# A gated cross-attention kernel on one core: the projections' matmuls spread over the whole attention

## What is computed

```python
# layer 0: cross-attention, 16 heads of 16, with pruned columns
q, k, v = ln(x) @ Wq.T + bq, ctx @ Wk.T + bk, ctx @ Wv.T + bv
s = softmax(q @ k.T / 4)                  # per head, 512 x 512
keep = top_k(s.sum(over queries), 460)    # 52 of 512 columns are dropped
x = x + tanh(g) * ((s * mask(keep)) @ v) @ Wo.T
x = x + tanh(g) * fp4_mlp(ln(x))          # 704 hidden, 16-element blocks
# layer 1: attention without softmax: q (k'v) needs only one 256 x 256 matrix
x = x + ...ln(x) @ (Wq1 @ blockdiag(k'v))...
x = x + tanh(g) * int8_linear(ln(x))
```

## Time and profile before

| | |
|---|---|
| median of 3 runs | 1215.02 us |
| times of the runs | 1215.01, 1215.02, 1220.33 us |
| span of the profiled execution | 1211.1 us |
| its busy time: TensorE, VectorE, ScalarE, GpSimd | 997.9, 1013.7, 935.9, 163.6 us |

### The profile page before, as it was taken

The page is one execution under the profiler, slowest core; times in us unless marked ns, Lnnn a source line. Parts: engine busy times, 40 slices in busy tenths (PEclk is TensorE's granted clock), DMA queues, the critical chain, the costliest instruction groups (busy, mean ns, idle before and its releaser), DMA issues.

```text
span 1211.1 us, 17973 instructions
## 1 busy us (share of the span) xinstructions
PE 997.9 (82%) x5672; PEld 476.7 (39%) x5672; DVE 1013.7 (84%) x2009; ACT 935.9 (77%) x2135; POOL 163.6 (14%) x183
## 2 busy tenths in 40 slices
PE   7888999967777677777777778998999999999974
PEld 5554556511111111111111111335677777767652
DVE  6887677788889888889888887567999999999965
ACT  5456565489999999999999998776567667766744
POOL 2221231020000000000000000101232222222212
PEclk9999999989999999999999999989999999999985
DMA  9730653042211222111223101101111211110001
GB/s 308 180 114 1 200 149 104 19 123 38 39 27 34 45 45 45 33 31 29 44 46 80 33 20 35 37 9 40 53 36 36 62 44 36 49 48 27 18 18 35
DMA packets 77906, 71.80 MB, mean 59 GB/s; under 512 B 13754, under 2 KB 71412, under 8 KB 77812
## 3 DMA queue, kind: packets, MB, share of 16 engines
q1 hardware_dynamic: 77812, 70.65, 22.2%
HBM read 42.83 MB, written 27.28 MB: 58 GB/s over the span
## 4 chain that ended last, share of the span: by engine, by line
PE 42%; ACT 39%; issue 9%; DVE 9%; DMA 0%; POOL 0%; ACTq 0%; DVEq 0%
ACT ea L1322 19%; ACT prob L1336 15%; PE ps_a L1598 13%; PE ps_b L1556 8%; PE ps_v L1556 3%; DVE nmax L1223 2%; PE ps_c L1571 2%; PE ps_a L1607 2%; PE ps_c L1632 1%; PE ps_v L1195 1%; PE ps_b L760 1%; PE ps_v L735 1%; PE ps_b L701 1%; PE ps_b L1146 1%; PE ps_c L1179 1%
## 5 line engine op out<-in xcount | busy, mean ns | idle before, releaser
L1322 ACT ACTIVATE ea<-ps_a,nmax 128x512 f32<-128x512 f32 x512 | 362.7, 748 | 72.2 <-DVE nmax L1223 72.2
L1223 DVE TENSOR_REDUCE nmax<-ps_a 128x2 f32<-128x1024 f32 x256 | 313.7, 1225 | 52.7 <-PE ps_a L1146 51.4
L1336 ACT ACTIVATE prob<-ps_b 128x1024 f32<-128x1024 f32 x214 | 236.1, 1103 | 0.0
L1146 PE MATMUL ps_b<-q_st,k_st 52*128 52x512 f16 x512 | 105.8, 391 | 137.7 <-ACT prob L1336 129.6
L1146 PEld LDWEIGHTS ps_b<-q_st,k_st 52*128 52x128 f16 x512 | 26.1, 93 | 364.2 <-ACT prob L1336 303.9
L1598 PE MATMUL ps_a<-wgu,xT 128*128 128x352 f32 x512 | 166.2, 465 | 3.4 <-ACT xT L1761 2.1
L1195 PE MATMUL ps_v<-prob,v_in 128*16 128x512 f32 x1024 | 135.5, 600 | 11.9 <-DVE att L1290 11.5
L1179 PE MATMUL ps_c<-ea,rz 128*32 128x512 f32 x1024 | 137.2, 608 | 0.0
L1322 ACT ACTIVATION_READ_ACCUMULATOR ea<-ps_a,nmax 128x1 f32 x512 | 135.8, 265 | 0.0
L1598 PEld LDWEIGHTS ps_a<-wgu,xT 128*128 128x128 f32 x512 | 92.9, 191 | 48.9 <-issue 7.0
L1773 ACT ACTIVATE ea<-ps_a 128x352 f32<-128x352 f32 x128 | 59.7, 467 | 59.1 <-PE ps_a L1598 58.7
(11 more groups left out here) (279 smaller groups left out, 1685.8 us busy)
## 6 DMA issues: line engine op xcount, KB each, us to landing
k_scr<-k_p SPq DMA_DIRECT2D x24, 256.0 KB, 2.9
q_scr<-q_p SPq DMA_DIRECT2D x24, 256.0 KB, 2.8
q_st<-q_scr SPq DMA_DIRECT2D x32, 192.0 KB, 4.8
k_st<-k_scr SPq DMA_DIRECT2D x32, 192.0 KB, 5.0
c_in<-in_ctx SPq DMA_DIRECT2D x8, 512.0 KB, 4.4
x_in<-in_x SPq DMA_DIRECT2D x8, 512.0 KB, 5.9
v_scr<-v_s SPq DMA_DIRECT2D x8, 512.0 KB, 3.1
v_in<-v_scr SPq DMA_DIRECT2D x16, 256.0 KB, 3.2
```

Source lines behind the costliest of these rows:

```text
L1146: return e.matmul(bank, left[b][o:o + rows, r, t * P:t * P + P], right[b][o:o + rows, r], start=True, stop=True)
L1223: e.tensor_reduce(nmax[u % 2][:, t].rearrange("p (h r) -> p r h", h=2)[:, r], ps_a[:, z % 2 * 2:z % 2 * 2 + 2], AX_X, ALU.max, negate=True ...
L1322: e.activation(ea[c % RING][:, g % 4], ps_a[:, g % 4], ACT.Exp, bias=nmax[u % 2][:, t, n:n + 1], accum_out=tot[u % 2][:, t, n:n + 1]).then ...
L1336: e.activation(dst, ps_b[:, :, :], ACT.Exp).then_inc(s_prob, 1)
```

## The change

Five things are changed together.

1. A fill is now done on TensorE in parts: X1, Q, K and V in two, GRAM in four, the others whole. Of the 187 parts that follow the first twenty fills, 67 are spread over half steps 0 to 40 (BEFORE, OPEN), and 120 over half steps 41 to 211, 0.7 per half step (RATE). Parts from z = 41 on use one bank of their own, `ps_f`. ScalarE empties a fill that ends at z at its step z - 1 (`leaving`), VectorE at step z (`ended`), GpSimd at z.
2. Column sums and values share one bank, `ps_s`: sums in partitions 0 to 63, values in 64 to 127. In every half step two matmuls of the sums and two of the values are issued, next to each other, where before four of the one or of the other were. The values' operand is 32 columns wide and half zeros (`v_pad`), written by GpSimd (`pad`).
3. ScalarE writes Q and K with their bias as float32 (`full`), and GpSimd splits them (`halves`: a copy and a subtraction, both 128x512). VectorE's `low_part` is gone.
4. `second` comes a half step later (z - 43), and ahead of the sums and values in TensorE's step. On VectorE the copy of the values moves to the head of a step, and the reciprocals go ahead of the ranking.
5. Buffers and DMA order: one `c_in` instead of two, one `q_p`, `k_p`, `v_s`, `m_s`; three `prob` instead of four; SP goes half step by half step, and loads a unit's heads 6 half steps ahead of their use. The dropped columns take 2 DMAs a unit instead of 4, the results 4 instead of 8. Fp4 work is dealt out over other fills of batches 1 to 3.

The core of the diff:

```diff
+    BEFORE, RATE = 67, 0.7
+    def bank_of(s):
+        return s % BANKS if s < alone else BANKS - 1
+    def parts(n):
+        if n >= 0 and n % FILLS in (X1, Q0, Q1, K0, K1, V0, V1):
+            return 2
+        return 4 if n >= 0 and n % FILLS == GRAM else 1
+    pieces = [(s, part) for s in range(AHEAD, len(SEQ)) if real(SEQ[s]) for part in range(parts(SEQ[s]))]
+    def turn_of(j):
+        if j < BEFORE:
+            return j * OPEN // BEFORE
+        return OPEN + int((j - BEFORE) / RATE)
...
+        def halves(dst, x, c, b, stored, done):
+            if b:
+                e.wait_ge(stored, OUT * b)
+            e.tensor_copy(dst[:, 0, c], x).then_inc(*po.up())
+            e.wait_ge(*po.now())
+            e.tensor_tensor(dst[:, 1, c], x, dst[:, 0, c], ALU.subtract).then_inc(done, 1)
...
-        def high_part(src, dst, bias, c):
-            return e.activation(dst[:, 0, c], src, ACT.Identity, bias=bias[:, c:c + 1])
+        def with_bias(src, n, bias, c):
+            j = QK.index(n)
+            for done, kinds in ((s_pool_q, (Q0, Q1)), (s_pool_k, (K0, K1))):
+                earlier = sum(x % FILLS in kinds for x in QK[:max(j - 1, 0)])
+                if earlier:
+                    e.wait_ge(done, earlier)
+            e.activation(full[j % 2][:, :], src, ACT.Identity, bias=bias[:, c:c + 1]).then_inc(s_act_full, 1)
...
+        def column_sums(g, k):
             u, n = g // GROUPS, g % GROUPS
+            t, r = n % TT, n // TT
             e.wait_ge(s_recip, g + 1)
+            if n == 0 and k == 0:
                 e.wait_ge(s_rank, u)
-            for j in range(4):
-                e.matmul(ps_c[32 * j:32 * j + 32, :], rz[:, n % TT, n // TT, j], ea[g % RING][:, j],
-                         start=(n == 0), stop=(n == GROUPS - 1)).then_inc(s_colsum, 1)
+            o = FIRST_ROW - 2 * r - k
+            for h in range(2):
+                e.matmul(ps_s[32 * h:32 * h + 32, :], rz[:, t, r, 2 * k + h, o:o + 32], ea[g % RING][:, 2 * k + h],
+                         start=(n == 0 and k == 0), stop=(n == GROUPS - 1 and k == 1)).then_inc(s_colsum, 1)
+        def values(g, k):
+            e.wait_ge(s_prob, 2 * g + k + 1)
+            if n == 0 and k == 0:
+                e.wait_ge(s_pad, u + 1)
+            if t == 0 and k == 0:
+                e.wait_ge(s_att, g // TT)
+            for h in range(2):
+                o = SUMS + 32 * h
+                e.matmul(ps_s[o:o + 32, :], v_pad[u % 2][:, t, 4 * r + 2 * k + h], at.prob[g % PROBS][:, 2 * k + h],
+                         start=(t == 0 and k == 0), stop=(t == TT - 1 and k == 1)).then_inc(s_value, 1)
         def step(z):
             if z < ALL_Z:
                 first(z)
-            if z % 2:
-                g = within((z - 5) // 2, ALL_G)
-                if g is not None:
-                    column_sums(g)
-            else:
-                g = within((z - LAG - 4) // 2, ALL_G)
-                if g is not None:
-                    values(g)
-            b = within(z - LAG, ALL_Z)
+            b = within(z - LAG - 1, ALL_Z)
             if b is not None:
                 second(b)
+            g = within((z - 4) // 2, ALL_G)
+            if g is not None:
+                column_sums(g, z % 2)
+            g = within((z - LAG - 4) // 2, ALL_G)
+            if g is not None:
+                values(g, z % 2)
...
+        def ended(z):
+            return pj.ends_at.get(z, ())
+        def leaving(z):
+            return [*(ended(z) if z <= pj.open else ()), *(ended(z + 1) if z >= pj.open else ())]
...
             for z in range(at.last):
                 step(z)
-                for n in fills(z):
-                    fill(n)
+                for s, part in pj.at_turn.get(z, ()):
+                    fill(s, part)
```

More of the change, by code:

```diff
@@ L177, in build @@
         fp4 = tiles.fp4
-        at = attend(m, w, scr, tiles)
+        at = attend(m, w, scr, tiles, fp4)
+        with ExitStack() as early:
+            fp4.wide_tiles(Mem(nc, early, ctx))
+        at.prob = [m.sb(f"prob{n}", [P, 4, T]) for n in range(at.probs)]
         with ExitStack() as early:
@@ L697, in transposes, with fill @@
             return ins
-        def into(dst, n, src, oc):
-            for ic in range(DC):
-                ins = e.matmul(dst, wt[:, n, ic, oc * P:oc * P + P], src[:, ic], start=(ic == 0), stop=(ic == DC - 1))
-            return ins
-        def fill(s):
-            n, dst = SEQ[s], bank[s % BANKS]
+        def fill(s, part):
+            n, dst = SEQ[s], bank[bank_of(s)]
             if not real(n):
                 return
-            g = s - BANKS
-            while g >= 0 and not real(SEQ[g]):
-                g -= BANKS
-            if g >= 0:
+            g = before(s)
+            if g >= 0 and part == 0:
                 e.wait_ge(*left(SEQ[g]))
@@ L717, in fill @@
             p = b % 2
+            last = part == parts(n) - 1
             if k in (CT0, CT1):
@@ L746, in fill @@
                 e.wait_ge(s_act_cT, 2 * b + 2)
-                into(dst, WK, cT, k - K0).then_inc(s_pe_k, 1)
+                oc = k - K0
+                ins = e.matmul(dst, wt[:, WK, part, oc * P:oc * P + P], cT[:, part], start=(part == 0), stop=last)
+                if last:
+                    ins.then_inc(s_pe_k, 1)
             elif k == KV:
@@ L787, in fill, with whole, stats, variances @@
                 e.wait_ge(s_act_xT, 2 * b + 2)
-                into(dst, WQ, xT, int(k == Q1)).then_inc(s_pe_q, 1)
-        return fill
+                oc = int(k == Q1)
+                ins = e.matmul(dst, wt[:, WQ, part, oc * P:oc * P + P], xT[:, part], start=(part == 0), stop=last)
+                if last:
+                    ins.then_inc(s_pe_q, 1)
+        def whole(s):
+            for part in range(parts(SEQ[s])):
+                fill(s, part)
+        return fill, whole
     def vector(e):
         dv = w.dve
-        def stats(b):
+        def stats(b, t0, t1):
             p = b % 2
             e.wait_ge(ey.s_x[p], 16 * (b // 2 + 1))
-            for t in range(TT):
+            for t in range(t0, t1):
                 e.bn_stats(st[p][:, t], ey.x_in[p][:, t]).then_inc(*dv.up())
+        def variances(b):
+            p = b % 2
             e.wait_ge(*dv.now())
```

578 lines of the change are left out of this document (312 added, 266 removed).

## The result

The changed kernel takes 1252.49 us (median of 4 runs, 1251.27 to 1255.39) against 1215.21 us for the kernel before on the same chip (4 runs): a ratio of 1.030, 95% interval 1.0276 to 1.0324. It is **slower by 3%**. I had forecast 1184, with 0.18 on slower.

A forecast was written before the change was run, and what follows sets the result against it. The opening was taken as bound by TensorE, the steady part by ScalarE. From a span of 1211.1 us: minus 84 (opening), plus 43 (steady part), plus 10 (tail) gives 1180, plus 3.9 gives 1184; 8 in 10 for 1156 to 1222.

The forecast's parts named there:

- The opening: Half steps 0 to 42: fills leave TensorE, whose sum falls to 106 us; stage takes 125, gain 84 (59 to 104).
- The opening isn't TensorE's: Rival, chance 0.10: opening is a chain of fills and emptying, 4.0 us a half step, gaining 41; 1227 us in all.
- The steady part: Half steps 42 to 211 take the fills that left the opening and are ScalarE's: loss 43 us (33 to 85).
- ScalarE's fill work: Steady part: ScalarE's added fill work, 33 us, all on the path; a half step goes from 2.26 to 2.46.
- Late fills, 0.06 per half step, 10 us: Steady part: waits for fills that end late cost 0.06 a half step, 10 us; bounds 0 and 0.3.
- mixed group: Sums and values, two and two in one bank, overlap like four strips, 1.07 us per half step: no cost.
- the bound of 2.46: Steady part: ScalarE's half step of 2.46 us, which TensorE at 2.17 and VectorE at 2.21 don't pass.
- GpSimd: The split of Q and K, 1.8 us 32 times, 57 us, is hidden; contention with VectorE lies inside the 10.
- The tail: Values alone, two abreast: 7 us in half steps with the feed's products, 3 elsewhere; loss 10 (2 to 19).
- Slower, the chain: Rival, chance 0.11: VectorE and TensorE in one loop with ScalarE, lumpy fills; middle half step 2.75, 1224 us in all.
- break-even: The gain turns into a loss when a middle half step takes more than 2.70 us.
- my own sign of being wrong: Prediction is wrong if middle half steps take 2.7 us or more; one of three such signs.

The follow-up runs named there:

- experiment 4: Changed kernel with all parts of fills done in half steps 0 to 40, in the three banks as before the change: 1271.51 us, 1.0468.
- experiment 12: experiment 10's kernel with the fills' matmuls left out from half step 41 on, except XT and CT: 1168.35 us, 0.9598.
- experiment 3: Changed kernel with ScalarE emptying a fill in the step in which it ends, between its exponentials, from z = 41 on: 1238.14 us, 1.0189.
- experiment 5: Changed kernel with both order edits, the ranking's copy ahead of the maxima and ScalarE's emptying between its exponentials: 1206.82 us, 0.9931.
- experiment 1: Changed kernel with the copy that opens a unit's ranking moved ahead of the maxima in VectorE's step: 1229.41 us, 1.0119.
- experiment 8: experiment 6's kernel with 29 parts moved back from the middle to the opening (BEFORE, RATE = 96, 0.545): 1203.83 us, 0.9893.
- experiment 7: Changed kernel with the split of queries and keys on VectorE instead of GpSimd: 1294.19 us, 1.0624.
- experiment 10: experiment 6's kernel with ScalarE's feed pieces in the tail one half step earlier: 1183.04 us, 0.9732.
- experiment 9: experiment 5's kernel with ScalarE's feed pieces in the tail one half step earlier: 1197.22 us, 0.9844.
- experiment 6: experiment 5's kernel with four strips again for sums of units 0 and 1 and for values from half step 262 on: 1201.11 us, 0.987.

## Why the prediction was wrong

**The opening: the number right, by two errors that cancel.** 76.9 of the forecast 84, and the stage shrank because TensorE's work left it, as I had said. *The opening isn't TensorE's* would have given 41. But TensorE's sum came out at 118, not 106, and the fullest engine was busy 0.90 of the stretch (118.1 of 132), as before the change, where I had put 0.84 because two engines are tied. That the two make 129 us together, near my 125, is luck. The sums took 43.3 us for my 37: a pair costs all of a four, 1.07 to 1.13, not 0.98. The Trainium skill (TensorE: Matmul & The Clock Gate, Measured speedup vs the span model) puts a pack of tiles at one matmul's time and about 4 ns more for each further tile, so that two cost what four do; the row of experiment 4 (45.07 for 20.89) and the tail's 1.05 for four records as for eight agree with it, and by it I had written 41. The rest is parts: 118.1 less 43.3 and 17.4 of scores leaves 57 for them, where I had 51.4. Their own records in the steady part take 1.09 us each, 130.4 for 120, where I had divided my way to 0.82 (143 by 176 is 0.81). ScalarE came out at 87 for my 85, in which I had put 6 for fp4 where the row says 4.1; VectorE at 110 for 105.

**The steady part: this failed.** The sum had two terms, and a third that I had put at nothing.

- *ScalarE's fill work*, forecast 33: measured 40 (424 busy in the middle for 383.5). Mis-sized a little, the mechanism right: in experiment 12, where TensorE's share is out, the half step is 2.51, and ScalarE is busy for 98% of it.
- *Late fills, 0.06 per half step, 10 us*: this is the step that failed most. ScalarE was idle 51 us in the middle, and over the steady part it stood 22.6 us for fills alone, where I had allowed 10. I had seen that "`leaving` empties a bank a half step before the others would, right behind a fill of up to 0.94 us", and priced it without walking through the order. `second` releases its exponential and the sums together, some 1.05 us on ScalarE and 1.07 on TensorE, and the part of 1.1 us begins only behind the sums; where ScalarE is not late itself, it must stand for most of a part that it empties (0.75 us on average in 30 of 47 cases). Mending that place gave back 14 us alone (experiment 3) and 23 on top of the ranking's edit (experiment 5 against 1).
- *What I had priced at nothing*: the sums of a new unit now fall in the very step whose VectorE part frees their bank, behind the maxima. I named the reciprocals' new place and found the mixed group free of cost, and didn't check the start of a unit. 30.1 us of TensorE's waiting, most of ScalarE's 21 us of waiting for `second`'s scores (6 in experiment 1), 23 us of time, and a stretch at half clock behind ten of the 13 waits in the steady part.

With both orders mended the middle lost 57 us, not 93: 40 of ScalarE's work and 17 of its idle time. Leaving out the parts' matmuls takes 15 off (experiment 12), 11 of them idle time and 4 busy. My averages for the other two engines were 2.17 us a half step for TensorE and 2.21 for VectorE; in the mended kernel they are 2.38 and 2.23 (404.6 and 378.7 of 442), so TensorE was nearer to the bound of 2.46 than I had it, by parts of 1.09 us instead of 0.82. And a part's price grows with their density, 0.37 us for the first 91 and 0.83 for the last 29 (experiment 8), which a sum of averages could not show.

**The mixed group: right.** The groups overlap; experiment 4 has the middle at 2.32 with the shared bank, and its two units without a slow stretch take 36.4 us for 36.2.

**GpSimd: right, as far as shown.** Its work is hidden; maxima keep their 1221 ns (1225 before), and experiment 7 shows no gain without it.

**The tail: the term right, another missing.** Pairs cost 11.9 us (experiment 10 against 9), 8 of them in the products' half steps; I had 10 and 7. But I had followed only the values' place in the tail. `second` moved by a half step past the feed's products and their emptying, and I did not follow that step past each queue: the loop of 3.4 us. That is the 10 of experiment 9, and it hid the pairs' cost at the same time, which is why experiment 6 found so little. 10.2 + 11.9 of the 24.8; about 3 stay unexplained.

**The rivals.** *Slower, the chain* had the right stage and nearly the right number (2.75 a half step; measured 2.81) at a chance of 0.11, and only half of the mechanism: the parts are lumps in one loop, as I put it there, but what made the lumps dearest was two places of the order, not an average load of 0.85. My break-even was 2.70, and my own sign of being wrong, middle half steps of 2.7 or more, came true. That the mended version runs at 1183 us and I forecast 1184 vindicates nothing: it has four strips back at the ends and three edits of the order.

## What to carry to other kernels

When a step moves by half a period, write down for every engine's in-order queue what now stands directly ahead of the instruction that frees its operand or its bank, at the start of a unit and in the tail as well as in the steady state. Work that "has slack on average" can still stop another engine, if the one that empties a bank is asked for it at the place where the filler is least likely to be done (here 0.75 us of waiting at a part of 1.1). Work that is moved into a stage has no fixed price either: here the last 29 parts cost over twice as much each as the first 91. And look twice at the saving of a packed group: in these kernels half of the strips cost the whole group's time (1.05 us for two as for four), unless another group filled the rest.

## What the runs showed of the hardware that I had not expected

- In the changed kernel a pause of TensorE of 1.68 us was followed by 3.4 us at a granted clock of 0.53, in which two of the sums' records took 1.07 instead of 0.62 us. The same pause doesn't always bring it: in experiment 4 ten of twelve waits of 1.11 us had a slow stretch behind them and two had none, and only there is its price seen by itself, 0.6 to 1.0 us. The middle had 0.96 on average; with the waits at the unit starts and ScalarE's waits shortened it had 1.00.
- Less work for TensorE did not keep the clock: with the fills' matmuls out it was 0.94 in the middle at 344.8 busy of 427 us, against 1.00 at 404.6 of 442; and yet the kernel before had 0.99 at 272.5 of 384. The share of busy time in the whole stage doesn't order them.
- ScalarE's own instructions were longer in the kernel before, where it was never idle, than after: 128x1024 exponentials 1103 ns on average, 1048 after; the two of 128x512 759 and 710. The records of neighbours overlap, and more so before: those of the exponentials and of their sums add up to 540 us in 384 us of busy time before (254 to 638 us), and to 495 in 393 after (175 to 650). So a shorter record here is no shorter half step.
- The contention that I read beside GpSimd before the change is rare: of the 39 instances of that VectorE product of 128x4 (L1944) one took 1.12 us, the other 38 0.16 to 0.17.
